# Halves of the first expert block's two way-in weights, and their low parts ahead of a table

## The chip, the cores and the metric

The kernel runs on one core of a Trainium2 chip. The metric is the device time of one execution in microseconds (us).

## What is computed

Four layers in a row on 4096 tokens of 256 numbers (8 sequences of 512), all in float32: an attention over the heads of each token, a quantised feed-forward layer, a cross attention with a mask, and at the end a mixture of experts, which is where the change lies:

```python
logits = x @ gate_w + gate_b                 # 8 experts
probs = jax.nn.softmax(logits)
top_w, top_idx = jax.lax.top_k(probs, 2)     # each token goes to 2 experts
top_w = top_w / jnp.sum(top_w, axis=-1, keepdims=True)
...
h = jax.nn.silu(x @ w1[e]) * (x @ w3[e])     # way in, 256 -> 1024, twice
out_e = h @ w2[e]                            # way out, 1024 -> 256
out = sum of the token's two out_e, weighted by combine
```

## The kernel before

The expert layer (function `experts`) works on blocks of 256 rows (`BLK`), each block with one expert; tokens have been scattered by expert into a table in memory, `expert_in`. The first two blocks (`KNOWN = 2`) belong to the expert with the most tokens and are known early; for the other 37 a small table (`first_row`, `expert`) says where a block's rows begin and which expert it has. VectorE computes that table on one partition in some forty short operations, the wide ones on 592 numbers.

One block goes like this. SyncE's queue (SP) loads its x rows (`m_x`) and its three weights w1, w3, w2 of 1 MB each into `raw[0..2]` (`m_raw`). The raw tiles are single: each reload waits until VectorE has finished with the earlier contents (`lo_done[n]`). Every float32 product is made of three faster ones, for which each factor is split: ScalarE writes the high part (`high_part`, tiles `m_hi`, `m_lo` for even blocks and `e_hi`, `e_lo` for odd ones, numbered 0 to 2 for w1, w3, w2), VectorE the low part as raw minus high (`low_part`). TensorE turns x (`turn`), then makes the way in (`hidden`): for each of 8 tiles f of the hidden width 12 products, 6 with w1 and 6 with w3, into four PSUM banks in turn, so that f = 4 and later wait for the gated tile f - 4. ScalarE takes the silu of the w1 half, VectorE multiplies it with the w3 half (`gated`), ScalarE takes the high part of a pair of gated tiles and VectorE the low part (`remainder`). `project` is the way out, in four quarters of 12 products, one for each pair.

Each engine runs its own list in the order in which the code writes it. In ScalarE's list the high parts of the next block's three weights stand behind the silus 1, 3 and 5; in VectorE's list the low parts of the next block stand in `gate` behind the gated tiles of pair 0 and pair 2, the third one in `slot`. Semaphores join the lists: `hi_done[n]`, `lo_done[n]` and `w_raw_in[n]` count these parts and landings, `gated_done`, `g_parts` and `silu_done` the steps in a block. At the seam TensorE makes 16 products of the identity with itself ("idle products"), once the first high part is done, so that its clock is up when the real ones begin.

Of the kernel before, what the change touches and what calls it, by code (L numbers as in the profile page):

```python
# [7 lines left out]
F32, BF16, F16, F8 = mybir.dt.float32, mybir.dt.bfloat16, mybir.dt.float16, mybir.dt.float8e4  # L8
F32R = mybir.dt.float32r
I32, U32 = mybir.dt.int32, mybir.dt.uint32  # L10
ALU, ACT, AX = mybir.AluOpType, mybir.ActivationFunctionType, mybir.AxisListType

P = 128
# [1673 lines left out]
def at_slot(i, q):  # L1687

    return ROUND * i + q
# [6 lines left out]
def tiles_in(q):  # L1696
    return 1 if q % ROUND in HALVES else BT
# [13 lines left out]
def experts(nc, M1, X, ident_f, routing, xs, out):  # L1711
# [10 lines left out]
    with ExitStack() as ctx:  # L1722
# [13 lines left out]
        w_raw_in = [sem(f"w_raw_in{n}") for n in range(3)]  # L1736
        hi_done, lo_done = [sem(f"hi_done{n}") for n in range(3)], [sem(f"lo_done{n}") for n in range(3)]
        h_ps, y_ps = sem("h_ps"), sem("y_ps")
        xb = two("x", [P, BT, WIDE])
# [9 lines left out]
        def load_weights(sp, i, q):  # L1749

            j, k = at_slot(i, q), table_index(i, q) - KNOWN
            known = isinstance(k, int) and k < 0
            e = sp.value_load(routing.first[0:1, 0:1] if known else expert[0:1, k:k + 1] if isinstance(k, int)  # L1753
                              else expert[0:1, bass.ds(k, 1)], min_val=0, max_val=NE - 1)
            for n, w in enumerate((w1, w3, w2)):
                if not (isinstance(j, int) and j == 0):
                    sp.wait_ge(lo_done[n], j)
                sp.dma_start(raw[n][:, :, :], w[e].rearrange("(c p) n -> p c n", p=P)).then_inc(w_raw_in[n], 16)  # L1758
# [7 lines left out]
        def low_part(eng, j, p, n):  # L1766
            eng.wait_ge(hi_done[n], j + 1)
            eng.tensor_tensor(w_lo[p][n][:, :, :], raw[n][:, :, :], w_hi[p][n][:, :, :].bitcast(F32), ALU.subtract)\  # L1768
                .then_inc(lo_done[n], 1)

        rows = out.rearrange("b s d -> (b s) d")

        with ExitStack() as run:
# [48 lines left out]
            g_high, y_left, y_out = sem_("g_high"), sem_("y_left"), sem_("y_out")  # L1822
            labelled, blanks, before_in = sem_("labelled"), sem_("blanks"), sem_("before_in")
            passed = sem_("passed")
# [27 lines left out]
            def _(pool):  # L1852
# [34 lines left out]
                for p in range(2):  # L1887
                    pool.memset(yb[p][:, :, :], 0.0).then_inc(blanks, 1)
                pool.wait_ge(blanks, 2)
                for q in range(ROUND):  # L1890
# [12 lines left out]
            def _(pe):  # L1903
# [17 lines left out]
                def hidden(i, q):  # L1921
                    j, p, wide = at_slot(i, q), q % 2, tiles_in(q) * P
                    for n in range(2):
                        pe.wait_ge(lo_done[n], j + 1)
                    pe.wait_ge(x_lo_done, j + 1)
                    for f in range(FC):
                        if f >= 4:
                            pe.wait_ge(gated_done, FC * j + f - 3)
                        for n, at in ((0, 0), (1, BLK)):
                            for c in range(KC):  # L1930
                                mm = three_passes(ps_h[f % 4][:, at:at + wide],
                                                  [w[p][n][:, c, f * P:(f + 1) * P] for w in (w_hi, w_lo)],
                                                  [x_hi[p][:, c, 0:wide], x_lo[p][:, c, 0:wide]], c == 0, c == KC - 1)
                        mm.then_inc(h_ps, 1)
# [15 lines left out]
                turn(0, 0)  # L1950
                pe.wait_ge(hi_done[0], 1)
                for _ in range(16):
                    pe.matmul(ps[:, 7, 0:P], ident_f[:, :], ident_f[:, :], start=True, stop=True)  # L1953
# [16 lines left out]
            def _(act):  # L1970
# [25 lines left out]
                x_high(0, 0)  # L1996
                for n in range(3):
                    high_part(act, 0, 0, n)
                for q in range(ROUND):
# [12 lines left out]
            def _(dve):  # L2012
# [11 lines left out]
                def gate(i, q, following=True):  # L2024

                    j, p, wide = at_slot(i, q), q % 2, tiles_in(q) * P
                    for k in range(FC // 2):
# [9 lines left out]
                        if k in (0, 2) and following:  # L2037
                            low_part(dve, j + 1, 1 - p, k // 2)
                    remainder(j, FC // 2 - 1, wide)

# [21 lines left out]
                def do(ins):  # L2062

                    steps.done(ins)
                    steps.wait()
# [24 lines left out]
                do(dve.tensor_scalar(weight[:, 1, NE - 1:NE], size[:, 0, NE - 1:NE], -1.0, None, ALU.mult))  # L2090
                wide = lambda a: a[:, :, :].unsqueeze(2).broadcast_to([1, 2, LISTED, NE])
                do(dve.tensor_tensor(past[:, :, :, :], limit[:, :, :].unsqueeze(3).broadcast_to([1, 2, LISTED, NE]), wide(now), ALU.is_ge))
                do(dve.tensor_reduce(n_past[:, :, :], past[:, :, :, :], AX.X, ALU.add))
# [13 lines left out]
                dve.tensor_scalar(expert[:, :], n_past[:, 0, :], float(NE - 1), None, ALU.min).then_inc(blocks_known, 1)  # L2107
                x_low(0, 0)
                for n in range(3):
                    low_part(dve, 0, 0, n)  # L2110
                for q in range(ROUND):
# [89 lines left out]
```

## Time and profile before

| | |
|---|---|
| median of 3 runs | 2061.55 us (2059.53 to 2062.30) |
| profiled execution, its own time | 2063.94 us |
| its span in the trace | 2062.2 us |
| TensorE busy | 1892.7 us, 92% |
| VectorE busy | 1552.3 us, 75% |
| ScalarE busy | 1145.8 us, 56% |
| expert blocks begin | about 1375 us |

Times in the trace count from the start of the span. Busy shares are means over layers with different limits, so for a change at one place the order of events at that place is what to read. PE is TensorE, ACT ScalarE, DVE VectorE, POOL GpSimd, and SPq the queue of SyncE, which issues the loads.

### The profile page before, as it was taken

To read this page: it belongs to the slowest core of one execution; us is meant where nothing else is said; L and a number is where in the kernel's file an instruction comes from. 1 tells how busy PE (TensorE), PEld (TensorE's weight loads), DVE (VectorE), ACT (ScalarE), POOL (GpSimd) and SP (SyncE) were. 2 spreads that over 40 slices of the span, in tenths; PEclk is the share of its full clock that TensorE was granted. 3 is DMA by queue.
4 is the path that set the end of the run, shared out by engine and by line. 5 is a ranking of instruction groups with operands and counts; after the bars stand their busy time and mean duration, and the time that the engine had idled before them with its cause. 6 is when DMAs were issued, how large, how long until landed. Compare 5 with 4: busy or idle time off the path is not lost. (4 is left out here: it accounts for less than half of the span.)

```text
span 2062.2 us, 35515 instructions
## 1 busy us (share of the span) xinstructions
PE 1892.7 (92%) x12100; PEld 1339.9 (65%) x12100; DVE 1552.3 (75%) x3251; ACT 1145.8 (56%) x2414; POOL 935.7 (45%) x674
## 2 busy tenths in 40 slices
PE   4899999986889999998999999959999999999998
PEld 2566776664543434443434343449999999999998
DVE  7999999992566677777767678657777777777785
ACT  2356666655336555555555555516665665656563
POOL 6999999981633334343534351023222231222322
PEclk9999999997999999999999999979999999999999
DMA  5222222210425051524242423037666666666662
GB/s 176 114 93 114 91 113 114 108 37 1 116 65 124 27 129 53 123 68 108 68 110 73 104 92 77 19 108 251 238 224 234 229 230 209 226 226 231 231 226 89
DMA packets 138569, 271.45 MB, mean 132 GB/s; under 512 B 13244, under 2 KB 90256, under 8 KB 132499
## 3 DMA queue, kind: packets, MB, share of 16 engines
q1 hardware_dynamic: 127916, 243.63, 37.9%
q0 software_dynamic: 9952, 25.25, 3.3%
q8 instruction: 99, 1.62, 0.3%
q14 instruction: 84, 0.68, 0.1%
q10 hardware_dynamic: 518, 0.27, 0.0%
HBM read 200.12 MB, written 70.47 MB: 131 GB/s over the span
## 5 line engine op out<-in xcount | busy, mean ns | idle before, releaser
L1476 DVE CUSTOM_DVE_ANT_0 x_dump<-x_ps,x_bias_q 128x512 bf16<-128x512 f32 x512 | 353.1, 690 | 103.0 <-PE x_ps L1160 90.1
L1345 ACT ACTIVATE x_PT<-x_ps 128x512 f32<-128x512 f32 x512 | 292.2, 601 | 230.6 <-PE x_ps L1175 227.4
L1989 ACT ACTIVATE X<-m_ps 128x256 f32<-128x256 f32 (+1 forms) x312 | 113.1, 363 | 222.0 <-PE m_ps L1918 219.6
L1160 PE MATMUL x_ps<-x_KS,x_QS 96*128 96x512 bf16 x512 | 198.1, 387 | 23.1 <-DVE x_mx L1476 22.2
L1872 POOL DMA_INDIRECT out_dram<-e_y,e_label x71 | 71.6, 1008 | 321.6 <-DVE e_y L2051 302.2
L1174 PE MATMUL x_ps<-x_bias_k,x_ident_b 128*128 128x512 bf16 x512 | 196.6, 384 | 2.8 <-DMA x_QS<-x_rows 1.7
L1175 PE MATMUL x_ps<-x_QS,x_KS 98*128 98x512 bf16 x512 | 196.5, 384 | 0.0
L1918 PE MATMUL m_ps<-e_x_lo,m_hi 128*128 128x256 f32 (+1 forms) x640 | 180.1, 281 | 4.5 <-issue 4.5
L1918 PE MATMUL m_ps<-e_x_hi,m_hi 128*128 128x256 f32 (+1 forms) x640 | 180.0, 281 | 0.0
L1918 PE MATMUL m_ps<-e_x_hi,m_lo 128*128 128x256 f32 (+1 forms) x640 | 179.9, 281 | 0.0
L2033 DVE TENSOR_TENSOR X<-X,m_ps 128x256 f32<-128x256 f32 (+1 forms) x312 | 114.0, 394 | 83.8 <-ACT X L1989 80.0
L1864 POOL DMA_INDIRECT e_y<-out_dram,e_label x71 | 101.8, 1434 | 164.8 <-DMA out_dram<-e_y,e_label 83.2
L296 POOL TENSOR_TENSOR a_pool_pv<-a_e,a_v 128x2304 f32<-128x2304 f32 x32 | 162.8, 5087 | 16.0 <-ACT a_e L478 16.0
L1918 PE MATMUL m_ps<-e_x_hi,e_hi 128*128 128x256 f32 (+1 forms) x608 | 169.8, 279 | 0.0
L1918 PE MATMUL m_ps<-e_x_hi,e_lo 128*128 128x256 f32 (+1 forms) x608 | 169.5, 279 | 0.0
L1918 PE MATMUL m_ps<-e_x_lo,e_hi 128*128 128x256 f32 (+1 forms) x608 | 169.5, 279 | 0.0
L1768 DVE TENSOR_TENSOR m_lo<-m_raw,m_hi 128x2048 fp32r<-128x2048 f32 x60 | 137.3, 2288 | 28.8 <-ACT m_hi L1764 28.8
L1768 DVE TENSOR_TENSOR e_lo<-m_raw,e_hi 128x2048 fp32r<-128x2048 f32 x57 | 130.4, 2287 | 26.8 <-ACT e_hi L1764 26.8
L1160 PEld LDWEIGHTS x_ps<-x_KS,x_QS 96*128 96x128 bf16 x512 | 50.1, 98 | 135.5 <-DVE x_mx L1476 104.9
L1918 PEld LDWEIGHTS m_ps<-e_x_lo,m_hi 128*128 128x128 f32 x640 | 121.8, 190 | 4.6 <-issue 4.6
L1918 PEld LDWEIGHTS m_ps<-e_x_hi,m_lo 128*128 128x128 f32 x640 | 121.8, 190 | 0.0
L1918 PEld LDWEIGHTS m_ps<-e_x_hi,m_hi 128*128 128x128 f32 x640 | 121.7, 190 | 0.0
(344 smaller groups left out, 5413.5 us busy)
## 6 DMA issues: line engine op xcount, KB each, us to landing
m_raw<-in_L_ffn_w_dram SPq DMA_DIRECT2D x117, 1024.0 KB, 5.1
expert_in<-a_blank SPq DMA_DIRECT2D x34, 1032.0 KB, 4.4
parts<-x_part SPq DMA_DIRECT2D x24, 512.0 KB, 3.8
m_x<-expert_in SPq DMA_DIRECT2D x32, 258.0 KB, 4.9
next_mask_k<-in_maskT_dram SPq DMA_DIRECT2D x32, 256.0 KB, 2.6
next_mask_q<-in_mask_dram SPq DMA_DIRECT2D x29, 256.0 KB, 2.8
x_KS<-parts SPq DMA_DIRECT2D x16, 384.0 KB, 11.3
x_QS<-parts SPq DMA_DIRECT2D x8, 576.0 KB, 6.7
```

Source lines behind the costliest of these rows:

```text
L296: pool.tensor_tensor(heads(pool_pv[:, :], PV_POOL), probabilities(e_[t % 2][:, PV_OWN * H:], PV_POOL), values(v_sb[t % 3][:, :], PV_POOL), ...
L1160: pe.matmul(ps_max[m % 2], QS[b % 2][0:HROWS, h, q * P:(q + 1) * P], KS[b % 2][0:HROWS, h, :], start=True, stop=True).then_inc(s1_ps, 1)
L1174: pe.matmul(ps_st[e % 3], ident_b[:, :], bias_k[b % 2][:, kc, :], start=True, stop=False)
L1175: pe.matmul(ps_st[e % 3], KS[b % 2][:, h, kc * P:(kc + 1) * P], QS[b % 2][0:HROWS + MROWS, h, :], start=False, stop=True).then_inc(st_read ...
L1345: act.activation(PT[unit % 2][:, k, :], ps_st[e % 3], ACT.Exp, scale=DH ** -0.5).then_inc(exp_done, 1)
L1476: dve.tensor_tensor_reduce(out=dump[:, :], in0=ps_max[m % 2], in1=bias_q[b % 2][:, q, :], scale=1.0, scalar=NEG, op0=ALU.add, op1=ALU.max, ...
L1768: eng.tensor_tensor(w_lo[p][n][:, :, :], raw[n][:, :, :], w_hi[p][n][:, :, :].bitcast(F32), ALU.subtract)\
L1864: pool.indirect_dma_start(out=yb[p][:, n, :], out_offset=None, in_=rows, in_offset=tokens(p, n), bounds_check=T - 1, oob_is_err=False).the ...
L1872: pool.indirect_dma_start(out=rows, out_offset=tokens(p, n), in_=yb[p][:, n, :], in_offset=None, bounds_check=T - 1, oob_is_err=False).the ...
L1918: mm = pe.matmul(out, left[a], right[b], start=first and n == 0, stop=last and n == 2)
L1989: act.activation(silu[f % 2][:, 0:wide], ps_h[f % 4][:, 0:wide], ACT.Silu).then_inc(silu_done, 1)
L2033: dve.tensor_tensor(gated[k % 2][:, n, 0:wide], silu[n][:, 0:wide], ps_h[f % 4][:, BLK:BLK + wide], ALU.mult)\
```

## The change

For block 0 alone, w1 and w3 are loaded and split by halves of their 1024 columns, in the order first half of w1, of w3, second half of w1, of w3; w2 stays whole. TensorE begins block 0 when both first halves are split, and asks for the second halves ahead of f = 4. VectorE makes the low parts of the first halves ahead of the wide operations of the table, those of the second halves behind the table, and that of w2 within block 0, behind the remainder of pair 0. The idle products are 14 instead of 16 and wait for nothing. Since w1 and w3 now count one step more in block 0, later waits on their counts are raised by one (`EXTRA`).

```diff
+        half_in = sem("half_in")
+        EXTRA = (1, 1, 0)
+        HALVES_OF = (slice(0, FF // 2), slice(FF // 2, FF))
...
+            if isinstance(j, int) and j == 0:
+                for h in HALVES_OF:
+                    for n, w in enumerate((w1, w3)):
+                        sp.dma_start(raw[n][:, :, h], w[e].rearrange("(c p) n -> p c n", p=P)[:, :, h])\
+                            .then_inc(w_raw_in[n] if h.start else half_in, 16)
+                sp.dma_start(raw[2][:, :, :], w2[e].rearrange("(c p) n -> p c n", p=P)).then_inc(w_raw_in[2], 16)
+                return
             for n, w in enumerate((w1, w3, w2)):
-                if not (isinstance(j, int) and j == 0):
-                    sp.wait_ge(lo_done[n], j)
+                sp.wait_ge(lo_done[n], j + EXTRA[n])
                 sp.dma_start(raw[n][:, :, :], w[e].rearrange("(c p) n -> p c n", p=P)).then_inc(w_raw_in[n], 16)
...
         def low_part(eng, j, p, n):
-            eng.wait_ge(hi_done[n], j + 1)
+            eng.wait_ge(hi_done[n], j + 1 + EXTRA[n])
...
+        def first_high(act):
+
+            for h in HALVES_OF:
+                for n in range(2):
+                    act.wait_ge(*((w_raw_in[n], 16) if h.start else (half_in, 32)))
+                    act.activation(w_hi[0][n][:, :, h], raw[n][:, :, h], ACT.Copy).then_inc(hi_done[n], 1)
+            high_part(act, 0, 0, 2)
+
+        def first_low(dve, h):
+
+            for n in range(2):
+                dve.wait_ge(hi_done[n], 2 if h.start else 1)
+                dve.tensor_tensor(w_lo[0][n][:, :, h], raw[n][:, :, h], w_hi[0][n][:, :, h].bitcast(F32), ALU.subtract)\
+                    .then_inc(lo_done[n], 1)
...
                 def hidden(i, q):
                     j, p, wide = at_slot(i, q), q % 2, tiles_in(q) * P
+                    first = isinstance(j, int) and j == 0
                     for n in range(2):
-                        pe.wait_ge(lo_done[n], j + 1)
+                        pe.wait_ge(lo_done[n], 1 if first else j + 2)
                     pe.wait_ge(x_lo_done, j + 1)
                     for f in range(FC):
+                        if first and f == FC // 2:
+                            for n in range(2):
+                                pe.wait_ge(lo_done[n], 2)
...
                 turn(0, 0)
-                pe.wait_ge(hi_done[0], 1)
-                for _ in range(16):
+                for _ in range(14):
                     pe.matmul(ps[:, 7, 0:P], ident_f[:, :], ident_f[:, :], start=True, stop=True)
...
                 x_high(0, 0)
-                for n in range(3):
-                    high_part(act, 0, 0, n)
+                first_high(act)
...
                         if k in (0, 2) and following:
                             low_part(dve, j + 1, 1 - p, k // 2)
+                        if isinstance(j, int) and j == 0 and k == 1:
+                            low_part(dve, 0, 0, 2)
...
                 wide = lambda a: a[:, :, :].unsqueeze(2).broadcast_to([1, 2, LISTED, NE])
+                x_low(0, 0)
+                first_low(dve, HALVES_OF[0])
                 do(dve.tensor_tensor(past[:, :, :, :], limit[:, :, :].unsqueeze(3).broadcast_to([1, 2, LISTED, NE]), wide(now), ALU.is_ge))
...
                 dve.tensor_scalar(expert[:, :], n_past[:, 0, :], float(NE - 1), None, ALU.min).then_inc(blocks_known, 1)
-                x_low(0, 0)
-                for n in range(3):
-                    low_part(dve, 0, 0, n)
+                first_low(dve, HALVES_OF[1])
```

The rest of the change replaces the semaphore `blanks` of GpSimd's two clearings by further counts of `iotas`.

VectorE's list, from the last short operations of the table on. `X` rows on one partition (1x...) are the table, m_lo_0 to m_lo_2 the low parts of block 0. Before:

```order
L2090 TENSOR_SCALAR X<-X 1x1
L2092 TENSOR_TENSOR X<-X 1x592
...
L2107 TENSOR_SCALAR m_expert<-X 1x37
L2018 TENSOR_TENSOR e_x_lo<-m_ps,e_x_hi 128x512
L2022 COPY e_label<-m_x 128x4
L1768 TENSOR_TENSOR m_lo_0<-m_raw,m_hi_0 128x2048
L1768 TENSOR_TENSOR m_lo_1<-m_raw,m_hi_1 128x2048
L1768 TENSOR_TENSOR m_lo_2<-m_raw,m_hi_2 128x2048
L2033 TENSOR_TENSOR X<-X,m_ps 128x256 x2
```

The same place now:

```order
L2118 TENSOR_SCALAR X<-X 1x1
L2044 TENSOR_TENSOR e_x_lo<-m_ps,e_x_hi 128x512
L2048 COPY e_label<-m_x 128x4
L1792 TENSOR_TENSOR m_lo_0<-m_raw,m_hi_0 128x2x512
L1792 TENSOR_TENSOR m_lo_1<-m_raw,m_hi_1 128x2x512
L2122 TENSOR_TENSOR X<-X 1x592
...
L2137 TENSOR_SCALAR m_expert<-X 1x37
L1792 TENSOR_TENSOR m_lo_0<-m_raw,m_hi_0 128x2x512
L1792 TENSOR_TENSOR m_lo_1<-m_raw,m_hi_1 128x2x512
L2059 TENSOR_TENSOR X<-X,m_ps 128x256 x2
```

The second pair of low parts, on which the reload of the raw tiles waits, now stands behind the wide operations, and m_lo_2 is gone from here.

VectorE's list in block 0, from its first gated pair (`X<-X,m_ps`) on, now; e_lo_0 and e_lo_1 are low parts of block 1, e_g_lo the remainders:

```order
L2059 TENSOR_TENSOR X<-X,m_ps 128x256 x2
L1777 TENSOR_TENSOR e_lo_0<-m_raw,e_hi_0 128x2048
L2059 TENSOR_TENSOR X<-X,m_ps 128x256 x2
L2071 TENSOR_TENSOR e_g_lo<-X,e_g_hi 128x512
L1777 TENSOR_TENSOR m_lo_2<-m_raw,m_hi_2 128x2048
L2059 TENSOR_TENSOR X<-X,m_ps 128x256 x2
L2071 TENSOR_TENSOR e_g_lo<-X,e_g_hi 128x512
L1777 TENSOR_TENSOR e_lo_1<-m_raw,e_hi_1 128x2048
```

The rows are those of before but for m_lo_2, which has come in between the first remainder and the third gated pair.

ScalarE's list in block 0, now: `X<-m_ps` are the silus, e_hi_0 to e_hi_2 the high parts of block 1.

```order
L1773 ACTIVATE m_hi_2<-m_raw 128x2048
L2016 ACT_TABLE_LOAD
L2016 ACTIVATE X<-m_ps 128x256 x2
L1773 ACTIVATE e_hi_0<-m_raw 128x2048
L2016 ACTIVATE X<-m_ps 128x256
L2006 ACTIVATE e_g_hi<-X 128x512
L2016 ACTIVATE X<-m_ps 128x256
L1773 ACTIVATE e_hi_1<-m_raw 128x2048
L2016 ACTIVATE X<-m_ps 128x256
L2006 ACTIVATE e_g_hi<-X 128x512
L2016 ACTIVATE X<-m_ps 128x256
L1773 ACTIVATE e_hi_2<-m_raw 128x2048
```

Nothing has moved here; the list is that of before from its m_hi_2 on.

## Rows read from the trace of the kernel before

**Rows 1.** The page: busy time of TensorE and its granted clock in 40 slices

```profile
PE 1892.7 (92%) x12100; PEld 1339.9 (65%) x12100; DVE 1552.3 (75%) x3251; ACT 1145.8 (56%) x2414; POOL 935.7 (45%) x674
...
PEclk9999999997999999999999999979999999999999
```

**Rows 2.** Chain that ended last, in time: start, us, what

```profile
1378.29 8.34 DMA m_raw<-in_L_ffn_w_dram
...
1388.62 6.79 PE m_ps L1953 x32
1395.40 11.52 PE m_ps L1918 x96
...
1407.36 17.01 PE m_ps L1918 x144
```

**Rows 3.** Timeline of TensorE at the first product of block 1: start, us

```profile
1412.90 0.28 PE L1918 MATMUL m_ps<-e_x_lo,e_hi 128*128 128x256 f32 x1
```

**Rows 4.** Timeline of VectorE at the seam: start, us, what [idle before it]

```profile
1380.54 0.76 DVE L2092 TENSOR_TENSOR X<-X 1x592 f32<-1x592 f32 x1
...
1386.29 0.17 DVE L2107 TENSOR_SCALAR m_expert<-X 1x37 int32<-1x37 f32 x1
1386.38 0.67 DVE L2018 TENSOR_TENSOR e_x_lo<-m_ps,e_x_hi 128x512 fp32r<-128x512 f32 x1
...
1388.60 2.29 DVE L1768 TENSOR_TENSOR m_lo<-m_raw,m_hi 128x2048 fp32r<-128x2048 f32 x1 [1.46 <-ACT m_hi L1764]
1391.21 2.29 DVE L1768 TENSOR_TENSOR m_lo<-m_raw,m_hi 128x2048 fp32r<-128x2048 f32 x1 [0.32 <-ACT m_hi L1764]
...
1400.55 2.29 DVE L1768 TENSOR_TENSOR e_lo<-m_raw,e_hi 128x2048 fp32r<-128x2048 f32 x1 [1.39 <-ACT e_hi L1764]
1402.76 0.74 DVE L2033 TENSOR_TENSOR X<-X,m_ps 128x256 f32<-128x256 f32 x2
1403.42 0.68 DVE L2043 TENSOR_TENSOR e_g_lo<-X,e_g_hi 128x512 fp32r<-128x512 f32 x1
```

**Rows 5.** Timeline of ScalarE at the seam, the same columns

```profile
1380.23 0.60 ACT L1974 ACTIVATE e_x_hi<-m_ps 128x512 fp32r<-128x512 f32 x1 [9.43 <-PE m_ps L1911]
1386.65 1.91 ACT L1764 ACTIVATE m_hi<-m_raw 128x2048 fp32r<-128x2048 f32 x1 [5.82 <-DMA m_raw<-in_L_ffn_w_dram]
...
1398.60 1.91 ACT L1764 ACTIVATE e_hi<-m_raw 128x2048 fp32r<-128x2048 f32 x1
...
1404.36 1.92 ACT L1764 ACTIVATE e_hi<-m_raw 128x2048 fp32r<-128x2048 f32 x1
1406.17 0.37 ACT L1989 ACTIVATE X<-m_ps 128x256 f32<-128x256 f32 x1
```

**Rows 6.** Weight loads issued from 1378 to 1380: issue ns, starts, time to landing

```profile
L1758 SPq DMA_DIRECT2D m_raw<-in_L_ffn_w_dram x3: 377/453/528, 1378.3 to 1379.3; - x3
...
DMA to landing us min/median/max: 8.3/10.5/12.6
```

**Rows 7.** The same, issued from 1390 to 1397

```profile
L1758 SPq DMA_DIRECT2D m_raw<-in_L_ffn_w_dram x3: 373/373/378, 1391.1 to 1396.2; - x3
...
DMA to landing us min/median/max: 5.9/6.5/6.8
```

**Rows 8.** The same, issued from 1403 to 1450

```profile
L1758 SPq DMA_DIRECT2D m_raw<-in_L_ffn_w_dram x9: 373/373/378, 1403.6 to 1447.7; - x9
...
DMA to landing us min/median/max: 4.8/5.0/7.0
```

**Rows 9.** Windows at TensorE's gap after 1728: busy of engines, granted clock, DMA

```profile
1728.00:1733.00 5.00, 0.83 (x8) 0.64 (x6) 2.84 (x4) 0.00 (x0) 1.00 (x1) 0.98 0.66 235
1733.00:1735.00 2.00, 1.68 (x8) 1.72 (x9) 0.00 (x0) 0.00 (x0) 0.00 (x0) 0.50 1.06 372
1735.00:1737.00 2.00, 2.00 (x14) 2.00 (x14) 0.25 (x1) 0.39 (x1) 0.00 (x0) 0.71 0.59 190
```

**Rows 10.** Window over the idle products, the same columns

```profile
1388.60:1394.50 5.90, 5.88 (x27) 5.89 (x28) 5.15 (x3) 4.41 (x3) 5.27 (x2) 0.50 0.66 202
```

More of the change, by code:

```diff
@@ L1822, in experts @@
             g_high, y_left, y_out = sem_("g_high"), sem_("y_left"), sem_("y_out")
-            labelled, blanks, before_in = sem_("labelled"), sem_("blanks"), sem_("before_in")
+            labelled, before_in = sem_("labelled"), sem_("before_in")
             passed = sem_("passed")
@@ L1887, in _ @@
                 for p in range(2):
-                    pool.memset(yb[p][:, :, :], 0.0).then_inc(blanks, 1)
-                pool.wait_ge(blanks, 2)
+                    pool.memset(yb[p][:, :, :], 0.0).then_inc(iotas, 1)
+                pool.wait_ge(iotas, 7)
                 for q in range(ROUND):
```

## The prediction

> **What bounds the kernel now.** I read the page first: TensorE is busy 92% of the span, and of 40 slices of granted clock two stand under 9, one of them at the seam between the attention layer and the expert blocks [rows 1]. Then the chain that ended last, in order of time, around that seam [rows 2]: from 1378.29 us it is the landing of the first weight (8.34 us), its high part on ScalarE (1.91 [rows 5]), the idle products (6.79) and from there TensorE alone, 144 products in 17.01 us or 0.118 us each, block after block. So whatever moves the first product of block 1 moves the end by as much, and whatever is done to block 0 without moving it is worth nothing. In this execution that product starts at 1412.90 [rows 3]. The sum below is the time of that one product.
>
> Then the timelines of VectorE [rows 4] and ScalarE [rows 5] there. VectorE works through the table from the first wide operation at 1380.54 to 1386.46 (1386.29 + 0.17), that is 5.92 us, while the weights are still coming; then x_lo (0.67) and the low parts, from 1388.60. The idle products end at 1395.4, while the second low part ends at 1391.21 + 2.29 = 1393.50 (2.29 is the mean of the one at 1388.60, the second follows it): about 1.7 us of product time lies under idle products now.
>
> **What the change gives at the start.** The halves of w1 and w3 come as 0.5 MB pieces in the order w1, w3, w1, w3. Today the first 1 MB is landed after 8.3 us, the next ones 10.5 and 12.6 us after their own issues 0.5 us apart [rows 6], which is 2.6 us for each MB, the third one (w2, whose rows are 1 KB instead of 4 KB) included; so shorter rows cost nothing, and two halves take the time of one whole: w3's first half lands at 1386.63, where w1 does now, the second halves near 1388.0 and 1389.3. High part of a half: the x tile of 512 columns took 0.60 us, 2048 columns 1.91 [rows 5], so 1024 take 1.04. Low part of a half: between 0.67 and 2.29 [rows 4], 1.21. First halves ready: 1386.63 + 1.04 + 1.21 + two hand-overs of 0.04 = 1388.95. Block 0 starts there and not at 1395.2, 6.2 us earlier. The 14 idle products take 14/16 of 6.79 = 5.9 us from about 1380.2 and end at 1386.1, hidden under the wait for the weights; they cost nothing, and without that cover they would cost these 5.9.
>
> **Where it is taken back.** The diff puts three things behind one another on VectorE that stood apart.
>
> 1. The wide part of the table (5.92) now runs after the first halves, as the order shows: 1388.95 to 1394.87. Then the low part of w1's second half, to 1396.08. TensorE's products after the first 48 want both second halves (1397.3) and the first gated tile (about 1397.7); before, they began at 1395.4 + 48 x 0.118 = 1401.1. If the kernel went on from there as before, 3.4 us would be left.
>
> 2. The raw tiles are single. SP reloads w1 for block 1 only when both low halves of w1 are done: 1396.15 with the hand-over, against 1391.06 before. Landing took 5.9 to 6.8 us for the three reloads issued between 1391 and 1396.2, each with another in flight [rows 7], and 4.8 to 7.0, median 5.0, later [rows 8]. This one has no weight before it, only scatters beside it: I take 5.6, keeping 4.8 and 6.8 as bounds. Landed 1401.75; e_hi_0 1.92, to 1403.7. In VectorE's order e_lo_0 stands ahead of the gated tiles 2 and 3 (it stood there before, but then ran at 1400.55 with its weight long there). It starts at 1403.7, 3.15 us later than before. What waits behind it: gated 2 and 3 and, through them, products of f = 6 and 7 on TensorE, and silu 4. From rows 4: the gated pair begins 2.21 after the start of e_lo_0 (1405.9), the remainder 0.66 later (1406.6).
>
> 3. w2's low part of block 0, ready long ago, is moved behind that remainder: start 1407.2, end 1409.5. The reload of w2 for block 1 waits for it: issued 1409.6 against 1396.2 before. ScalarE wants that reload for e_hi_2, which stands ahead of silu 6. With 5.0 us (nothing in flight but an x tile and later pieces; bounds 4.8 to 7.0) it lands at 1414.6. Before, e_hi_2 ran at 1404.36. Silu 6 follows 1.81 later [rows 5], 1416.4; gated 6 at 1416.8; ScalarE's high part of pair 2 and silu 7, gated 7 done 1418.0; remainder of pair 2 done 1418.65, of pair 3 1419.4. TensorE, which could do only the first half of block 0's way out by then (about 1413.5), starts the third quarter (12 products) at 1418.7, then the fourth: 24 x 0.118 = 2.8 us, 1421.5. That is 8.6 us later than 1412.90.
>
> The reload of w3 (issued about 1397.3) lands under the e_hi_0 stall. The two extra DMA issues on SP (about 0.4 to 0.5 us each) lie ahead of w2's first landing only, whose high part now has 15 us of cover. The pool's semaphore and the changed counts cost nothing: no engine does other work for them.
>
> **Clock.** TensorE stands idle from about 1400.5 (24 products after 1397.7) to 1406.3 and again from about 1414 to 1418.7. The trace has one such gap in the expert part: 0.83 us busy of the five after 1728, and behind it the granted clock is 0.50 for two microseconds and 0.71 on average for the next two [rows 9], so some 3 us at 1.2 GHz, in which half of the products' rate is lost: 1.4 us. I take 1.4 us once, for the second gap (what the first costs is hidden, since TensorE waits again). Bounds: 0, and 2.95, half of the 5.9 us at 0.50 that it took from 1388.6 [rows 10]. The Trainium skill (TensorE: Matmul & The Clock Gate, "HAM oscillation — how this bites in real kernels") says that waits for a transfer between bursts let the clock fall each time and that the next burst then starts cold; the trace agrees at its one gap, and by the rule the sum would be the same.
>
> **Sum.** 8.6 + 1.4 = 10.0 us slower. The other bounds: the two reloads at 4.8 and 4.8 give 1.0 less, at 6.8 and 7.0 give 3.2 more; if the first landing was late (8.3 us against 4.8 to 7.0 elsewhere) for a reason that doesn't strike small pieces, all moves up by up to 3.5. From block 1 on the order on each engine is that of before, and all is as late as the first product. This execution took 2063.94 us around its span of 2062.2, so 2073.9 for its like; it lies 2.4 above the median of the three runs, 2061.55, and so the forecast for the median is 2071.5.
>
> The Trainium skill (DMA: Bandwidth & Descriptors, "Anatomy of one DMA") gives about 2.0 us plus bytes over 436 GB/s for a DMA on GpSimd's path, an estimate of 4.4 us for 1 MB; by it the two reloads would cost 1.8 less and the sum be 8.2. No reload in this trace was that fast, the shortest being 4.8.
>
> **Rivals.** A measurement of this kernel can tell about 0.2%, 4.1 us, from no change.
> - *Both reloads bind* (above): 2068.5 to 2074, chance 0.62.
> - *Colder or slower*: the gap near 1414 leaves TensorE at 1.2 GHz for as long as the start at 1388.6 did, or the reloads take the upper bounds (they follow scatters and gathers): 10.0 + 1.5 + 2 is about 2075, chance 0.13. For it: the reloads at 5.9 to 6.8. Against it: the median of 5.0.
> - *One stall only, or an early first landing*: the w2 reload hides (then the first alone leaves 3.6 us: 8.6 without the 5.0 from 1409.6 to 1414.6) or the front moves up 3.5: 2065.5 to 2068, chance 0.15. Against the first: silu 6 stands behind e_hi_2 on ScalarE, and the 8.2 us that lay before between its reload's issue (1396.2) and its start (1404.36) are gone.
> - *Not slower*: the reloads are there when asked for, and the early start stays. It ends near 2060, since VectorE reaches block 0's first gated tile at 1397.3 as before and now has m_lo_2 (2.3) among them, so that of the 3.4 us won at product 48 about 1.1 is left. It decides where a landing takes under 2.5 us (1396.15 to the 1398.6 at which e_hi_0 began before); the minimum of all seen is 4.8. Chance 0.07; a gain over 4.1 us, with the full 6.2 kept (2055.4), 0.03.
>
> **How the numbers follow.** The range from 2065.5 to 2075.5 holds the first three nearly whole, without the last two and some of the second. Slower by over 0.2% (above 2065.7): 0.62 + 0.13 and nearly all of the 0.15, 0.88. Within 0.2%: 0.08 with what is left. Faster: 0.04.
>
> **What would show it.** In the changed kernel's profile: first real product near 1389 (right or wrong on the halves); VectorE idle before e_lo_0 until about 1403.7 behind ScalarE's e_hi_0, ScalarE idle before e_hi_0 and again some 6 us before e_hi_2 behind weight landings; TensorE with two idle stretches in block 0, both outlasting 4 us; the first product of block 1 near 1422.9. It is wrong if the reload of w1 is issued well before 1396, if e_hi_2 starts before 1410, or if later blocks win time back, which would mean that TensorE was not the bound there.

## The result

The changed kernel takes 2074.22 us in the median of five runs (2072.09 to 2076.20), the kernel before 2061.55 (2059.28 to 2063.67): a ratio of 1.0063, with a 95% interval of 1.0048 to 1.0077. It is 12.7 us slower, where 10.0 was forecast. Its profiled execution took 2076.17 us around a span of 2074.4.

The page of the changed kernel, the same lines as in [rows 1]:

```profile
PE 1902.6 (92%) x12096; PEld 1348.7 (65%) x12096; DVE 1552.0 (75%) x3253; ACT 1146.0 (55%) x2416; POOL 929.6 (45%) x674
...
PEclk9899999997999999999999999978999999999999
```

TensorE's records are as many as before but for the idle products, and it is busy 9.9 us longer: the same products, more of them at 1.2 GHz. At the seam two slices of granted clock stand under 9 where there was one. The chain that ended last shows the way there (start, us, what; compare [rows 2]):

```profile
1378.16 7.56 DMA m_raw<-in_L_ffn_w_dram
1385.74 1.06 ACT m_hi L1785
1386.83 2.36 DVE m_lo L1792 x2
1389.19 0.69 DVE X L2122
...
1395.58 0.17 DVE m_expert L2137
1395.76 1.14 DVE m_lo L1792
1397.06 4.82 DMA m_raw<-in_L_ffn_w_dram
1401.90 1.92 ACT e_hi L1773
1403.84 2.29 DVE e_lo L1777
...
1407.31 2.29 DVE m_lo L1777
1409.62 5.31 DMA m_raw<-in_L_ffn_w_dram
```

Before, the chain left the landing after one step and ran on TensorE alone. Now it goes from a landing through ScalarE and VectorE, over the whole table, and twice more over a landing. TensorE enters it at 1419.04, for the third quarter of block 0's way out. Its timeline (start, us, ..., idle before it and who ended it):

```profile
1389.29 0.55 PE L1942 MATMUL m_ps<-e_x_lo,m_hi 128*128 128x256 f32 x1 [4.39 <-issue]
...
1398.50 0.36 PE L1942 MATMUL m_ps<-e_x_lo,m_hi 128*128 128x256 f32 x1 [1.04 <-DVE X L2059]
...
1406.52 0.58 PE L1942 MATMUL m_ps<-e_x_lo,m_hi 128*128 128x256 f32 x1 [4.94 <-DVE X L2059]
...
1419.04 0.58 PE L1942 MATMUL m_ps<-m_lo,e_g_hi 128*128 128x256 f32 x1 [3.99 <-DVE e_g_lo L2071]
...
1424.33 0.41 PE L1942 MATMUL m_ps<-e_x_lo,e_hi 128*128 128x256 f32 x1
```

The last row is the first product of block 1, at 1412.90 before [rows 3]. The two idle stretches of 4.94 and 3.99 us are blamed on VectorE, since the gated tile and the remainder are what ended them. ScalarE's timeline names the ones that VectorE waited for itself (compare [rows 5], where neither row has an idle time before it):

```profile
1401.90 1.91 ACT L1773 ACTIVATE e_hi<-m_raw 128x2048 fp32r<-128x2048 f32 x1 [6.87 <-DMA m_raw<-in_L_ffn_w_dram]
...
1414.96 1.91 ACT L1773 ACTIVATE e_hi<-m_raw 128x2048 fp32r<-128x2048 f32 x1 [7.22 <-DMA m_raw<-in_L_ffn_w_dram]
```

And the windows over the second gap and behind it (PE busy and count, then the other engines; the last three numbers are granted clock, DMA share, GB/s), to be held against [rows 9]:

```profile
1414.00:1418.00 4.00, 1.05 (x9) 0.85 (x8) 0.46 (x2) 2.97 (x4) 0.00 (x0) 1.00 1.05 413
1418.00:1420.00 2.00, 0.96 (x4) 0.96 (x5) 1.91 (x4) 1.11 (x2) 0.00 (x0) 0.55 0.98 403
1420.00:1422.00 2.00, 2.00 (x12) 2.00 (x11) 2.00 (x3) 0.00 (x0) 0.00 (x0) 0.50 0.03 10
1422.00:1424.00 2.00, 2.00 (x11) 2.00 (x11) 1.12 (x2) 0.00 (x0) 0.00 (x0) 0.50 0.07 7
1424.00:1426.00 2.00, 2.00 (x15) 2.00 (x15) 0.48 (x1) 0.00 (x0) 0.03 (x1) 0.75 0.85 259
```

The 24 products from 1419.04 to 1424.33 took 5.3 us, where 24 x 0.118 = 2.8 is full speed.

**The yardstick.** The time at which the expert layer begins differs by several us from one execution to the next, with the same code ahead of it. So the experiments are read by the time from the issue of the first weight load to the first product of block 1, each from its own profile:

```
kernel                      issue     block 1   yardstick  to before  from high  median of all its runs, ratio (95%)
before                      1378.29   1412.90   34.61                 26.25      2061.55
before, second profile      1371.17   1403.36   32.19      -2.4       25.35
changed                     1377.68   1424.33   46.65      +12.0      38.59      2074.22, 1.0063 (1.0048 to 1.0077)
changed, second profile     1374.91   1421.11   46.20      +11.6      38.84
e1  w2's low part back      1375.75   1413.93   38.18      +3.6       30.17      2065.79, 1.0028 (1.0016 to 1.0040)
e2  w2 own memory           1380.54   1419.84   39.30      +4.7       31.67      2070.93, 1.0042 (1.0017 to 1.0067)
e3  w1, w2 own memory       1374.88   1412.89   38.01      +3.4       30.45      2064.39, 1.0011 (0.9992 to 1.0029)
e4  idle products in gap    1380.11   1424.77   44.66      +10.1      36.52      2076.74, 1.0080 (1.0063 to 1.0097)
e5  halves, table first     1377.61   1411.80   34.19      -0.4       25.97      2061.86, 1.0003 (0.9991 to 1.0014)
e6  idle products alone     1377.40   1411.70   34.30      -0.3       26.65      2063.29, 1.0000 (0.9986 to 1.0015)
e7  all halves ahead        1375.90   1412.53   36.63      +2.0       29.57      2061.63, 1.0002 (0.9991 to 1.0014)
e8  e5 + w1, w2 own memory  1385.01   1416.07   31.06      -3.6       22.79      2059.21, 0.9992 (0.9978 to 1.0006)
e9  e1 + w1, w3 own memory  1377.17   1412.91   35.74      +1.1       28.44      2065.62, 1.0020 (1.0005 to 1.0034)
e10 e8 + 36 idle products   1373.10   1404.38   31.28      -3.3       23.23      2062.53, 1.0000 (0.9986 to 1.0014)
```

"To before" is against 34.61, the profile on which the prediction rests. "From high" is the part of the yardstick from the start of block 0's first high part on ScalarE to the first product of block 1, so it leaves the first landing out. That is needed because the yardstick of the kernel before scatters by 2.4 us over its two profiles. Its second profile shows where (start, us, what):

```profile
1371.17 6.82 DMA m_raw<-in_L_ffn_w_dram
1378.01 1.92 ACT m_hi L1764
1379.98 5.90 PE m_ps L1953 x32
```

The landing took 6.82 us against 8.34 in [rows 2], and the idle products 5.90 against 6.79. From the high part on, two profiles of one kernel differ by 0.9 (before) and 0.25 us (changed). So a difference of under 2.5 us in the yardstick, or of under 1 us from the high part, is not read.

The ratios are each against runs of the kernel before beside it on the same chip; their intervals are 2 to 5 us wide on either side, so that the smaller steps are seen in the profiles only.

### The profile page after: what moved, and what is told of

Its sections match the earlier page's. It is cut to its first block and busy times, and to the rows that moved or that the text cites. A ratio compares the mean times of both kernels' runs of the same rounds, so it can differ in the third digit from the quotient of the medians.

```text
span 2074.4 us, 35524 instructions
## 1 busy us (share of the span) xinstructions
PE 1902.6 (92%) x12096; PEld 1348.7 (65%) x12096; DVE 1552.0 (75%) x3253; ACT 1146.0 (55%) x2416; POOL 929.6 (45%) x674
## 5 line engine op out<-in xcount | busy, mean ns | idle before, releaser
L1888 POOL DMA_INDIRECT e_y<-out_dram,e_label x71 | 99.6, 1403 | 164.1 <-DMA out_dram<-e_y,e_label 84.6
L1777 DVE TENSOR_TENSOR m_lo<-m_raw,m_hi 128x2048 fp32r<-128x2048 f32 x58 | 132.6, 2286 | 26.6 <-ACT m_hi L1773 26.6
```

The lines of the kernel that those rows point to most:

```text
L1888: pool.indirect_dma_start(out=yb[p][:, n, :], out_offset=None, in_=rows, in_offset=tokens(p, n), bounds_check=T - 1, oob_is_err=False).the ...
```

## The experiments

The theory on record: two reloads in a row come late, w1's because VectorE makes the second halves' low parts behind the table, w2's because its own low part has moved behind the first remainder; behind the second stall the clock is down. The rivals are the pieces of the change by themselves (halves, idle products, table ahead of gated tiles) and the place of w2's low part on VectorE without its reload.

### e1: the low part of w2 put back

```diff
-                        if isinstance(j, int) and j == 0 and k == 1:
-                            low_part(dve, 0, 0, 2)
...
                 first_low(dve, HALVES_OF[1])
+                low_part(dve, 0, 0, 2)
```

> The changed kernel with one part undone: the low part of w2 for block 0 stands right behind the second halves again, ahead of block 0's gated tiles. The theory (two reload stalls in a row, and a cold clock behind the second): the reload of w2 for block 1 is issued near 1400.3 us and has landed when e_hi_2 is wanted, so the second stall goes and the first stays; first product of block 1 near 1415.6 instead of 1424.3, some 8 to 9 us faster than the changed kernel, about 2065. Rival (the loss is the first stall, or the start, and the second wait lies beside it): no more than 3 us faster, 2071 or more.

ScalarE's high parts of block 1:

```profile
1400.04 1.92 ACT L1773 ACTIVATE e_hi<-m_raw 128x2048 fp32r<-128x2048 f32 x1 [7.14 <-DMA m_raw<-in_L_ffn_w_dram]
...
1405.79 1.91 ACT L1773 ACTIVATE e_hi<-m_raw 128x2048 fp32r<-128x2048 f32 x1
```

The first wait is there as in the changed kernel, the second is gone. The yardstick falls by 8.5 us to 38.18 (8.4 from the high part), the median by 8.4 us to 2065.79. The place of this one operation carries two thirds of the loss.

### e2: the reload of w2 made early, VectorE's order kept

Block 0's w2 is loaded into `X[:, 24:32, :]`, which nothing uses at that time, and split from there; SP's wait ahead of block 1's w2 is for the high part only.

```diff
+        OWN = (2,)
+        raw_of = lambda j, n: X[:, {0: 16, 2: 24}[n]:{0: 24, 2: 32}[n], :].rearrange('p a b -> p (a b)').rearrange('p (c n) -> p c n', n=shapes[n][-1]) if isinstance(j, int) and j == 0 and n in OWN else raw[n]
...
-                sp.wait_ge(lo_done[n], j + EXTRA[n])
+                sp.wait_ge(*((hi_done[n], 2 - n // 2) if isinstance(j, int) and j == 1 and n in OWN else (lo_done[n], j + EXTRA[n])))
```

> The changed kernel, with w2 of block 0 loaded into memory that is free then (rows 24 to 31 of X), so that the reload of raw[2] doesn't wait for the low part but for the high part. VectorE's order is that of the changed kernel. Theory: only the second stall goes; m_lo_2 and e_lo_1 still stand ahead of gated tiles, so the last quarter starts near 1415.7 and block 1 near 1416.5 to 1417, 7 to 8 us faster, about 2066.5. Rival (it is the place of m_lo_2 on VectorE that costs, not the reload that waits for it): 2 us or less faster, 2072.

e_hi_2 started with no idle time before it:

```profile
1410.10 1.90 ACT L1775 ACTIVATE e_hi<-m_raw 128x2048 fp32r<-128x2048 f32 x1
```

The yardstick is 39.30, 7.35 us less than in the changed kernel. What e1 has over it, 1.1 us (1.5 from the high part), would be the place of m_lo_2 on VectorE, the rival; it is too near the scatter to be given as a share, but the late reload holds most of the 8.5. The whole time shows less: the median of 2070.93 is 3.3 below that of the changed kernel, its interval overlaps that kernel's, and it is above the forecast 2066.5; this kernel's six runs lie between 2065.2 and 2075.1, and the profiled one began its expert layer 2.9 us later than the changed kernel's.

### e3: w1 of block 0 has its own memory too

The same edit for two weights:

```diff
-        OWN = (2,)
+        OWN = (0, 2)
```

> As e2, and w1 of block 0 too has its own memory (rows 16 to 23 of X), so that both reloads that ScalarE waits for come early. Theory: both stalls go, no clock is lost; what stays is m_lo_2 on VectorE within block 0 and the late start of its gated tiles at 1398.0. First product of block 1 near 1412.2, level with the kernel before: 2061.5, between 2060 and 2063. Rival (the early start of 6 us is kept once nothing stalls): 2057 or less. Rival (half loads, more issues or the table itself cost): 2065 or more.

A miss: level with before was expected, and the yardstick is 3.4 above (4.2 from the high part; 5.1 against the second profile of before). ScalarE shows why (its two idle times behind a landing):

```profile
1399.94 1.92 ACT L1775 ACTIVATE e_hi<-m_raw 128x2048 fp32r<-128x2048 f32 x1 [3.34 <-DMA m_raw<-in_L_ffn_w_dram]
...
1404.36 1.92 ACT L1775 ACTIVATE e_hi<-m_raw 128x2048 fp32r<-128x2048 f32 x1 [1.44 <-DMA m_raw<-in_L_ffn_w_dram]
```

e_hi_0 was early (1391.78), but w3 still waited for the low parts behind the table, and w2's reload is behind w3's on SP. I had written that w3's reload lies under the stall of w1's; with that cover gone it is itself the stall, 3.3 us. The stall had moved to the next load in the queue.

### e9: no reload late, the table still between the halves

e1's edit and memory of their own for w1 and w3 (rows 16 to 31 of X, so that `raw_of` has an entry for w3), w2's load as in the changed kernel:

```diff
-        OWN = (2,)
+        OWN = (0, 1)
```

> e1 with memory of its own for w1 and w3 of block 0, so that the wide table still stands between the halves, but no reload waits for anything late: w1's and w3's are asked for near 1389, w2's near 1400.3. Theory: no stall is left but the late start of the gated tiles near 1400.2 (2.2 us of w2's low part), so the yardstick is 35 to 35.5, half a us to 1 us slower than before and 3 us faster than e1. Rival (what is left in e1 is not the reload of w1): the yardstick stays at 38.2.

No high part of block 1 waited for its landing here: the 7.14 us of idle time ahead of e_hi_0 in e1 are gone. The yardstick is 35.74, 2.4 below e1 (1.7 from the high part). That is the first stall by itself, and it is small, since TensorE now idles 2.96 us until 1399.43 in any case, for gated tiles behind the table and w2's low part. What is left without any late reload is 1.1 us over the first profile of before, and 2.2 to 3.1 from the high part over its two. The whole time agrees that something is left, 1.0020 with an interval from 1.0005 to 1.0034, but doesn't show the step from e1, whose median is 0.2 us away.

### e7: all four halves ahead of the table

```diff
                 first_low(dve, HALVES_OF[0])
+                first_low(dve, HALVES_OF[1])
...
-                first_low(dve, HALVES_OF[1])
+                low_part(dve, 0, 0, 2)
```

(and no low part of w2 in block 0)

> The changed kernel with the low parts of all four halves ahead of the wide table, and w2's right behind it, none in block 0. The reloads of w1 and w3 are asked for near 1390.5 and 1391.6 as before, w2's near 1400.4. Theory: no reload is late for ScalarE; what is left is that block 0's gated tiles wait for the table (6.6 us) and w2's low part until 1400.3; yardstick 35 to 36.5, level with e9, where the reloads were made early in another way. Rival (not the reloads but the table ahead of the gated tiles is what costs in the changed kernel): 40 or more.

The yardstick is 36.63 and the ratio 1.0002. It is the same account by another way: the reloads of w1 and w3 are asked for from 1387.7 on, and 10 of the 12 us are gone (9.0 from the high part) with the table still ahead of the gated tiles. The rival (40 or more) falls. It is 0.1 above the expected range; TensorE idled 3.97 us until 1397.93, where block 0 then went on at 1.2 GHz.

### e5: halves and idle products alone

VectorE's order as before: the whole table, x_lo, the four halves, w2's low part.

```diff
-                x_low(0, 0)
-                first_low(dve, HALVES_OF[0])
...
+                x_low(0, 0)
+                first_low(dve, HALVES_OF[0])
                 first_low(dve, HALVES_OF[1])
+                low_part(dve, 0, 0, 2)
```

> The changed kernel with VectorE's order that of before: wide table first, then x_lo, the low parts of the halves, and w2's, all ahead of block 0's gated tiles. Halves of columns and the 14 idle products stay. Yardstick from here on: the time from the issue of the first weight load to the first product of block 1, 34.6 us before and 46.65 in the changed kernel. Theory (the table between the halves, and w2's low part behind them, make the reloads late; halves in themselves give time): table done near 1386 under the landings, low parts of all halves done near 1391.5, reload of w1 issued near 1390.4 as before; yardstick 31 to 33, 2 to 3 us faster than before, about 2060. Rival (halves or idle products without a wait cost in themselves): yardstick 36 or more.

The halves don't cost, but they hardly pay: yardstick 34.19, within the 32.2 to 34.6 of before, and 25.97 from the high part, within its 25.4 to 26.3, where a yardstick of 31 to 33 was expected. All that the change adds besides the order on VectorE is in this kernel, the semaphore of GpSimd too, and none of it shows as a loss. TensorE began at 1389.38, 11.8 us after the first issue (before 16.9), and it was out of work again ahead of f = 6. Windows over that, same columns as above:

```profile
1398.00:1401.00 3.00, 1.44 (x13) 1.24 (x11) 2.50 (x2) 3.00 (x5) 0.00 (x0) 1.00 1.04 387
...
1403.00:1405.00 2.00, 2.00 (x12) 2.00 (x11) 2.00 (x2) 2.00 (x3) 0.00 (x0) 0.50 0.96 392
1405.00:1408.00 3.00, 3.00 (x23) 3.00 (x23) 2.81 (x6) 1.94 (x4) 0.00 (x0) 0.85 0.51 135
```

Half of three us without work, and a little later the clock is at 1.2 GHz until about 1406. What I had left out of the forecast was this: the reload of w1 still binds (ScalarE idle 2.24 us ahead of e_hi_0), so an earlier first product only makes the gap ahead of f = 6 wider, and the gap has its own price in clock.

### e8: halves, table first, and the reloads early

e5's edit and e3's together:

```diff
+        OWN = (0, 2)
```

> e5 with memory of its own for w1 and w2 of block 0 (rows 16 to 31 of X), so that block 1's w1 and w2 are asked for as soon as block 0's high parts are made. Theory: what limits e5 is the landing of block 1's w1 ahead of the gated tiles 2 and 3; it now lands about 2 us sooner, and the yardstick is 30 to 31, 4 us faster than before. Rival (the limit in e5 is VectorE or the clock at 1.2 GHz over block 0's first products): the same as e5 within 0.5 us.

The yardstick is 31.06, at the upper edge of what was expected; from its first real product on TensorE has no idle stretch in block 0. From the high part it is 22.79, 2.6 and 3.5 below the two profiles of before, so here about half or more of the early start is kept. In the median of ten runs it is 2059.21, a ratio of 0.9992 with an interval from 0.9978 to 1.0006: the gain is in the profile, and one in the whole time is not shown.

### e6: the idle products alone

```diff
                 turn(0, 0)
-                pe.wait_ge(hi_done[0], 1)
-                for _ in range(16):
+                for _ in range(14):
```

(in the kernel before)

> The kernel before with one part of the change alone: 14 idle products right behind the turn of block 0's x and no wait for the first high part. Theory: TensorE then stands idle from about 1386 to 1393.5 and begins block 0 at 1.2 GHz, 1.7 us earlier than before; half clock for some 6 us costs 3, so yardstick 35.7 against 34.6, about 1 us slower. Rival (idle products by themselves are what the change gains): yardstick 33, 1.7 us faster.

The yardstick is 34.30, the ratio 1.0000. From the high part it is 26.65, 0.4 and 1.3 above the two profiles of before: the rival's gain is not there, and the loss of 1 us is neither shown nor excluded. TensorE began its products 14.3 us after the first issue instead of 16.9, and at 1.2 GHz until about 1397 (windows, same columns):

```profile
1388.00:1391.60 3.60, 0.00 (x0) 0.00 (x0) 3.56 (x2) 2.78 (x3) 3.00 (x2) 0.81 0.75 192
...
1395.00:1397.00 2.00, 2.00 (x11) 2.00 (x11) 0.42 (x1) 0.00 (x0) 1.45 (x2) 0.50 1.03 420
1397.00:1399.00 2.00, 2.00 (x19) 2.00 (x19) 0.42 (x1) 1.85 (x2) 0.00 (x0) 0.99 1.04 379
```

So the earlier start brings nothing that can be seen; that the lower clock takes it back fits these windows.

### e10: e8 with idle products up to the first real one

In e8:

```diff
-                for _ in range(14):
+                for _ in range(36):
```

> e8 with 36 idle products instead of 14, so that they reach from the turn of block 0's x to the first real product: e8's TensorE stood idle for 5.47 us there and began at 1.2 GHz. An idle product took 0.232 us at 2.4 GHz in e4. Theory (in e8 TensorE is never idle from its first real product on, so its clock over the first 3.3 us is now the bound): yardstick 29 to 30 against 31.06, 1 to 2 us faster than e8, 4 to 6 us faster than before, about 2057. Rival (a landing or a low part is the bound right behind, or the idle products hang over the first real one): yardstick 31 or more.

The rival's way: yardstick 31.28 against 31.06 (23.23 and 22.79 from the high part). The granted clock is 1.00 from 1380 on, so the idle products do what they are for, but the gated tiles are the bound right behind:

```profile
1391.14 0.36 PE L1944 MATMUL m_ps<-e_x_lo,m_hi 128*128 128x256 f32 x1 [0.51 <-DVE X L2061]
...
1394.82 0.39 PE L1944 MATMUL m_ps<-e_x_lo,m_hi 128*128 128x256 f32 x1 [0.59 <-DVE X L2061]
```

The whole time is that of before (1.0000). So no version here is shown to be faster than the kernel before in the whole time.

### e4: the second gap filled

```diff
                     for f0 in range(0, FC, 2):
+                        if isinstance(j, int) and j == 0 and f0 == 4:
+                            for _ in range(20):
+                                pe.matmul(ps[:, 0, 0:P], ident_f[:, :], ident_f[:, :], start=True, stop=True)
                         pe.wait_ge(g_parts, FC // 2 * j + f0 // 2 + 1)
```

> The changed kernel with 20 more idle products between the second and third quarter of block 0's way out, where TensorE has nothing to do for 4 us. They fill 1415.0 to 1419.2 at 2.4 GHz. Theory: the 24 products behind the gap take 2.9 us instead of 5.3 and block 1 starts at full clock, 2.5 to 3 us faster, about 2071.5. Rival (the clock is not what makes them slow, or it falls elsewhere): no gain, 2074 or later by the idle products' overhang.

In TensorE's timeline the third quarter starts at 1421.82, 41.7 us after the first weight issue (changed kernel 41.4), and block 1 2.95 us later instead of 5.29:

```profile
1416.70 4.63 PE L1972 MATMUL m_ps<-ident_f 128*128 128x128 f32 x40
...
1421.82 0.39 PE L1942 MATMUL m_ps<-m_lo,e_g_hi 128*128 128x256 f32 x1 [0.49 <-DVE e_g_lo L2074]
...
1424.77 0.28 PE L1942 MATMUL m_ps<-e_x_lo,e_hi 128*128 128x256 f32 x1
```

So what made the products behind the gap slow was the clock: with TensorE kept busy they take 2.3 us less, and the yardstick is 2.0 shorter (2.1 from the high part). The whole time doesn't show it: 2076.74 in four runs, 2.5 above the changed kernel instead of 2.5 to 3 below it, with overlapping intervals. In the profile the first issue came 2.4 us later than in the changed kernel's and what follows the first product of block 1 took 0.9 longer; that the added products cost anything elsewhere is not shown.

### Second profiles of both kernels

> The kernel before, unchanged, for a second profile: how far the yardstick (first weight issue to first product of block 1) and the rest scatter from one execution to the next. Theory: everything in the yardstick hangs on landings and engine times that agreed within a few tenths, so 34.6 within 0.7, while the time up to the first weight issue moves by several us as it did over the profiles so far (1373.1 to 1385.0). Rival (the yardstick scatters as much as the totals do, and no single profile can be read): off by 2 us or more.

> The changed kernel, unchanged, for a second profile. Theory: both stalls again, yardstick 46.65 within 1.5 (the clock behind the second gap may come back 1 or 2 us sooner or later). Rival: 43 or less, which would make half of the loss an accident of one execution.

32.19 and 46.20. The kernel before is 2.4 below its first profile, where 0.7 was allowed, and that is what the rival asked for. It doesn't scatter as the totals do, though: 1.5 of the 2.4 us are the first landing and 0.9 the idle products, both read above, and the rest repeats. This is why the table has the column from the high part. In the changed kernel both stalls are there again: ScalarE idles 7.91 and 7.08 us behind the two landings, and TensorE 4.57 us ahead of the third quarter. The loss is 12.0 us over the first profiles and 14.0 over the second ones; from the high part it is 12.3 and 13.5.

## Why the prediction was right

Like with like means time after the first weight issue (1378.29 before and in the forecast, 1377.68 now).

- **First product of block 0.** Forecast 10.7 after the issue, measured 11.6. The order of steps was wrong: the two first halves share one semaphore, so that w1's high part waits for both landings, and the second low part stands behind the first (the x2 of 2.36 us in the chain) instead of only one after the landing. The landings were a little earlier than forecast, 8.0 instead of 8.3.
- **The table.** Forecast 5.92, measured 6.64 (1389.11 to 1395.75), most of it one operation that took 0.83 us instead of 0.23. With it w1's reload is asked for 19.4 after the issue, forecast 17.9.
- **First reload.** 5.6 taken, 4.8 measured, the lower bound. e_lo_0 starts 26.2 after the issue, forecast 25.4.
- **Second reload.** Issued 31.9 after (31.3 forecast), landing 5.3 (5.0), e_hi_2 at 37.3 (36.3), third quarter at 41.4 (40.4). Every step of the chain that was written down is there, in that order, and all of it is about 1 us late. The steps missed by more than their sum: 0.9 for the first product, 0.6 for the table and 0.3 for the second reload's landing are what it took too little, 0.8 for the first reload's landing what it took too much. TensorE's two idle stretches are 4.94 and 3.99 us; both were to outlast 4. e1 and e2 show that the second wait is worth 7 to 8.5 us, clock included; e9 against e1 that the first is worth about 2 of what then is left, which is within the scatter of the yardstick. The sentence in which the w3 reload cost nothing was true of the changed kernel, and e3 shows what its cover was.
- **Clock.** This is the term that was mis-sized: 1.4 taken, 2.45 measured (5.29 - 2.84) up to block 1. I had read the recovery off one gap, which took 3 us; here TensorE stayed at 1.2 GHz for about 6 us, as it did at the idle products of [rows 10], which was the upper bound. e4 confirms the term by removing it. One gap was not enough to read it from. All four profiles of the two kernels have this same later gap, and the 96 products behind it took (before, before again, changed, changed again; from the chains that ended last):

```profile
1733.32 12.91 PE m_ps L1918 x96
1723.81 14.08 PE m_ps L1918 x96
1744.70 13.79 PE m_ps L1942 x96
1741.51 13.17 PE m_ps L1942 x96
```

  At 0.118 us each they would take 11.3, so the same gap costs 1.6 to 2.8 us, by the execution.
- **Sum.** 1.0 for the late front and 1.0 for the clock make the 12.0 of the yardstick out of 10.0. The two profiled executions differ by 12.2: the first issue is 0.6 earlier, and from the first product of block 1 to the end it is 650.07 us against 649.30. Those last 0.8 are scatter: the second profiles have it the other way round, 650.44 before and 649.49 in the changed kernel. "All is as late as the first product" holds within that. That the medians differ by 12.7 is inside the interval of the ratio, 10 to 16 us.
- **The rivals.** "Colder or slower" described the size better than the likeliest case did: 2074.2 is between the two. "One stall only" falls with e_hi_2, which waited 7.22 us for its landing, and "not slower" with the landings of 4.8 and 5.3 us, not under 2.5. That the size came out inside the range owes something to the first reload's landing, whose error went against those of the start and the table: that much is luck. The Trainium skill's formula (DMA: Bandwidth & Descriptors, "Anatomy of one DMA") gave an estimate of 4.4 for each; the measured 4.8 is nearer to it than my 5.6 was, the measured 5.3 is nearer to my 5.0, and both are above it.

## What to carry to other kernels

Before moving work that frees a buffer, ask who reloads the buffer, what stands behind the reloaded data on each in-order engine, and by how much the reload is ahead today: here a low part of 2.3 us was moved 13 us down the list, and a transfer of 5 us came onto the path behind it. A start that is 5.3 us earlier is worth nothing if the next refill of the same buffer is later; and a covered load that is taken out of a stall uncovers the next one in its queue (e3). A gap on TensorE is priced with the slow products behind it, and the time it takes to come back is read from more than one gap.

## What was not expected of the hardware

- After gaps of similar length the clock stayed at 1.2 GHz for very different times, though TensorE was busy throughout. Behind the gaps of 3.99 and 4.57 us in block 0 it was 6 us (after 1419 in the changed kernel) and 4.5 us (its second profile). Behind the one gap of 4.4 to 4.5 us that all four profiles have in a later block it was about 3 and 5 us in the kernel before and 4.5 and 3.5 us in the changed one. In e5 it fell behind a stretch in which TensorE had work in 1.44 of 3.00 us.
- The issue of the first weight load lay between 1371.2 and 1385.0 us over fourteen profiles with the same program ahead of it. What makes the layers before so uneven was not looked into.
- One 37-element operation of VectorE took 0.83 instead of 0.23 us while GpSimd was clearing its tiles. The fourteen profiles all fit: in the eight in which the clearing falls into the table, one such operation takes 0.83 to 1.50 us and ends within 0.05 us of the end of the clearing; in the other six the longest is 0.23. So it looks like a wait for GpSimd, but no run moved the clearing alone. Here it is 0.6 us of the table's 6.64.
